# Two expert stages of one kernel: a threshold search shared between VectorE and ScalarE, and the last expert's tail cut into halves

## The reference

```python
T = b * s                                   # 2048 tokens
C = int(T * F_C / E)                        # 256 places for each of 16 experts
scores = softmax(flat_x @ gate_w.T).T       # 16 x 2048
topk_weight, topk_idx = top_k(scores, C)    # the 256 best tokens of each expert
xg = flat_x[topk_idx]
h = gelu(xg @ Wg) * (xg @ Wu)               # 512 inner features
eo = (h @ Wd) * topk_weight
out = zeros.at[topk_idx].add(eo)
shared = (gelu(x @ Sg) * (x @ Su)) @ Sd     # 256 inner features, for all tokens
return out + shared                         # x = x + 0.5 * this
```

## Time and profile before

| | us |
|---|---|
| median of 3 runs | 1262.27 |
| lowest and highest of them | 1257.03, 1264.00 |
| the profiled execution, its own time | 1254.24 |
| its span, first to last instruction | 1252.4 |
| mean granted clock of TensorE, share of full | 0.962 |

### The profile page before, as it was taken

How to read it: one execution, slowest core, us unless ns; L and a number is a source line. 1 busy time by engine, 2 the same in 40 slices (tenths; PEclk the granted TensorE clock), 3 DMA queues, 4 the chain that set the end, 5 groups by cost and what they waited for, 6 DMA issues and landing times. The chain is left out here.

```text
span 1252.4 us, 19707 instructions
## 1 busy us (share of the span) xinstructions
PE 1143.5 (91%) x6507; PEld 567.8 (45%) x6507; DVE 857.6 (68%) x1893; ACT 702.6 (56%) x885; POOL 520.0 (42%) x544
## 2 busy tenths in 40 slices
PE   4799999999999998769997599999999999787998
PEld 1444444444444485358983122222222223446896
DVE  6466566666666555864425999999999995485441
ACT  3677777787787715312215266766777767531221
POOL 0066656656656700337862013223312311135884
PEclk9999999999999998879999599999999999797999
DMA  4001001001001010416754431322222130223765
GB/s 124 1 7 25 18 24 40 18 24 34 24 24 35 19 35 2 171 58 175 188 112 88 88 64 27 73 55 47 57 52 61 42 52 1 84 90 92 196 168 121
DMA packets 54603, 81.90 MB, mean 65 GB/s; under 512 B 18520, under 2 KB 36316, under 8 KB 53404
## 3 DMA queue, kind: packets, MB, share of 16 engines
q1 hardware_dynamic: 42392, 70.83, 21.1%
q0 software_dynamic: 10944, 8.92, 4.8%
q10 hardware_dynamic: 1192, 1.19, 0.3%
HBM read 55.34 MB, written 11.67 MB: 54 GB/s over the span
## 5 line engine op out<-in xcount | busy, mean ns | idle before, releaser
L1777 ACT ACTIVATE at_PR<-psum 128x1024 f32<-128x1024 f32 x256 | 248.0, 1021 | 123.3 <-PE psum L2006 123.0
L1845 DVE TENSOR_REDUCE at_MX<-psum 128x1 f32<-128x512 f32 x468 | 300.9, 685 | 11.0 <-PE psum L1988 6.6
L1714 POOL TENSOR_TENSOR at_PR<-at_PR,at_FAC 128x512 f32<-128x512 f32 x64 | 81.2, 1268 | 293.4 <-ACT at_PR L1777 293.4
L486 ACT ACTIVATE PR<-psum 128x1024 f32<-128x1024 f32 x144 | 141.0, 1026 | 82.1 <-PE psum L770 75.2
L770 PE MATMUL psum<-Q,K 64*128 64x512 f32 (+3 forms) x768 | 143.5, 502 | 1.2 <-ACT PR L486 1.2
L491 ACT ACTIVATE PR<-PR 128x1024 f32<-128x1024 f32 x144 | 144.5, 1062 | 0.0
L782 PE MATMUL psum<-PR,V 128*64 128x512 f32 (+3 forms) x768 | 139.7, 495 | 0.1
L2006 PE MATMUL psum<-at_QS,at_KS 122*128 122x512 bf16 x512 | 136.0, 387 | 2.2 <-DVE at_MX L1841 1.6
L2024 PE MATMUL psum<-at_PR,at_VG 128*32 128x512 f32 x1024 | 137.0, 608 | 0.0
L463 POOL TENSOR_SCALAR_AFFINE_SELECT PR<-PR 128x256 f32<-128x256 f32 (+1 forms) x112 | 58.1, 533 | 167.4 <-ACT PR L491 167.3
L1397 PE MATMUL psum<-moe_XGT,moe_WE 128*128 128x256 f32 x512 | 124.3, 388 | 0.6 <-ACT moe_XGT L1110 0.6
(11 more groups left out here) (238 smaller groups left out, 1629.4 us busy)
## 6 DMA issues: line engine op xcount, KB each, us to landing
moe_WE<-in_c_We SPq DMA_DIRECT2D x32, 768.0 KB
XB<-at_r_dram SPq DMA_DIRECT2D x32, 256.0 KB, 3.8
at_QS<-at_SPL SPq DMA_DIRECT2D x72, 64.0 KB
at_KS<-at_SPL SPq DMA_DIRECT2D x72, 64.0 KB
at_KS<-in_c_krows SPq DMA_DIRECT2D x8, 384.0 KB
moe_rows_dram<-XNS SPq DMA_DIRECT2D x2, 1152.0 KB, 10.4
moe_spare_dram<-moe_zeros SPq DMA_DIRECT2D x2, 1024.0 KB, 13.0
moe_sum_dram<-XB SPq DMA_DIRECT2D x2, 1024.0 KB, 3.8
```

Source lines behind the costliest of these rows:

```text
L486: act.activation(PR[u][:, :, :], S[(b + u) % 2][:, :, :], ACT.Tanh, scale=SCALE0 / CLAMP).then_inc(z.clamped, 1)
L1714: pool.tensor_tensor(pr, pr, FAC[:, 4 * (s // 2):4 * (s // 2) + 4, :], ALU.mult).then_inc(z.factored, 1)
L1777: act.activation(PR[:, gu % PRS, 2 * r:2 * r + 2, :].rearrange("p h n -> p (h n)"), g.psum[:, 2 * r * BANK:(2 * r + 2) * BANK], ACT.Exp).t ...
L1845: dve.tensor_reduce(MX[:, 4 * (2 * pair + c % 2) + I % 4, khalf:khalf + 1], bank(("max", c))[:, :], AX, ALU.max).then_inc(z.reduced, 1)
```

## The change

Five things. (1) ACT counts the third candidate (which is now the middle one in size) as the sum of signs of score minus candidate, over `S3`, a copy of the scores with the lowest bit set; scores are lifted by 2^26, and the candidate carries the sign bit as a negative bias. PE adds ACT's sum with a matrix of halves, after an offset product (`lifted`) in the same PSUM columns, which alternate between two banks. DVE counts two candidates. In step 0 alone DVE has two more passes: it makes `S3`, and counts the scores above zero (a fourth column). (2) Four `shared_in` stand ahead of the turn of the scores; the other twelve stand behind steps 0 to 7 (two behind even steps, one behind odd), `shared_x` and `shared_down` behind steps 8 to 14 and one part behind the search. ACT's Gelu, Copy and halving stand behind its sign of a given step; POOL's pieces may begin three steps earlier. (3) The last down product is made by halves of the inner features and leaves its two halves of rows in two banks, each with its own signal. (4) The mask products take one half of the rows after the other. (5) For quarters 2 and 3 of the tokens DVE and POOL add `LAST` to `g.X` (`merge`), and PE has two L1437 products instead of four.

```diff
+MULTIPLES, SIGN = np.array([1, 3, 2]), np.int64(-2 ** 31)
+LIFT = 26
...
+        def merge(eng, k, done):
+            eng.wait_ge(z.reloaded[k], 16)
+            eng.wait_ge(z.spared[k], 16)
+            eng.tensor_tensor(g.X[:, 4 * k:4 * k + 4, :], g.X[:, 4 * k:4 * k + 4, :], LAST[:, 4 * k:4 * k + 4, :], ALU.add).then_inc(done, 1)
...
             @block.gpsimd
...
-                    pool.wait_ge(z.stepped, o + 5)
+                    pool.wait_ge(z.stepped, o + 2)
...
+                merge(pool, 3, z.merged2)
...
             @block.scalar
...
+                gelu_at, copy_at, half_at = {1: 1, 4: 2, 7: 3}, {0: 0, 3: 1, 5: 2, 8: 3}, {10: 0, 12: 1, 14: 2}
+                shared_gelu(0)
+                act.wait_ge(z.odd, 1)
+                for i in range(SEARCH_STEPS):
+                    act.wait_ge(z.stepped, i + 1)
+                    with nc.allow_low_precision(reason="even integers up to 256"):
+                        act.activation(junk[:, TRIES - 1, :], S3[:, :], ACT.Sign, bias=cand[:, TRIES - 1:TRIES].bitcast(F32),
+                                       accum_out=cnt[:, TRIES - 1:TRIES]).then_inc(z.acted, 1)
+                    if i in gelu_at:
+                        shared_gelu(gelu_at[i])
+                    if i in copy_at:
+                        shared_copy(copy_at[i])
+                    if i in half_at:
+                        shared_half(half_at[i])
+                shared_half(3)
...
             @block.vector
...
-                ch(dve.tensor_copy(S2[:, :], ps[3][:, 0:CW]))
+                ch(dve.tensor_scalar(S2[:, :], ps[3][:, 0:CW], 2.0 ** LIFT, None, ALU.mult))
...
-                    for k in range(TRIES):
+                    for k in range(TRIES - 1):
                         last = dve.tensor_scalar(junk[:, k, :], S2[:, :], cand[:, k:k + 1].bitcast(F32), 0.0, ALU.is_ge,
                                                  ALU.add, accum_out=cnt[:, k:k + 1])
+                        if i == 0 and k == 0:
+                            dve.tensor_scalar(S3[:, :].bitcast(I32), S2[:, :].bitcast(I32), 1, None, ALU.bitwise_or).then_inc(z.odd, 1)
+                    if i == 0:
+                        last = dve.tensor_scalar(junk[:, TRIES, :], S2[:, :], 2.0, 0.0, ALU.is_ge, ALU.add,
+                                                 accum_out=cnt[:, TRIES:TRIES + 1])
...
-                rows_out(E1 - 1)
+                dve.wait_ge(z.scattered[lane(E1 - 1 - DEEP)], landed(E1 - 1 - DEEP))
+                dve.wait_ge(z.wcopied, E1)
+                for k in range(2):
+                    dve.wait_ge(z.down, E1 + k)
+                    dve.tensor_scalar(EO[:, (E1 - 1) % DEEP, k, :], ps[k][:, 0:D], WT[:, (E1 - 1) % DEEP, k:k + 1],
+                                      None, ALU.mult).then_inc(z.scaled, 1)
+                merge(dve, 2, z.merged)
...
             @block.tensor
...
+                for o in range(4):
+                    shared_in(o)
+                pe.wait_ge(z.permuted, 1)
...
+                lifted(0)
                 for i in range(SEARCH_STEPS):
+                    pe.wait_ge(z.acted, i + 1)
+                    pe.matmul(totals(i)[:, TRIES - 1:TRIES], g.half[:, :], cnt[:, TRIES - 1:TRIES], start=False, stop=False,
+                              skip_group_check=True)
                     pe.wait_ge(z.counted, i + 1)
...
-                    pe.matmul(ps[3][:, 256:256 + TRIES], same[:, :], cnt[:, :], start=True, stop=True).then_inc(z.totalled, 1)
+                    pe.matmul(totals(i)[:, 0:TRIES - 1], same[:, :], cnt[:, 0:TRIES - 1], start=False, stop=True,
+                              skip_group_check=True).then_inc(z.totalled, 1)
+                    if i + 1 < SEARCH_STEPS:
+                        lifted(i + 1)
+                    k = (i - 8) // 2
+                    if i < 8:
+                        for o in range(4 + (3 * i + 1) // 2, 4 + (3 * i + 4) // 2):
                             shared_in(o)
+                    elif i % 2 == 0:
...
                         shared_x(k)
                         shared_down(k, 0, 2)
+                    else:
                         shared_down(k, 2, 4)
...
+                shared_down(3, 2, 4)
...
-                down(E1 - 1)
+                pe.wait_ge(z.scaled, 2 * E1 - 2)
+                for h in range(2):
+                    pe.wait_ge(z.hidden, 2 * E1 - 1 + h)
+                    for k in range(2):
+                        last_down(h, k)
                 pe.wait_ge(z.masked, 9)
-                pe.wait_ge(z.scaled, 2 * E1)
-                for t in range(NT):
-                    for k in range(2):
+                for k in range(2):
+                    pe.wait_ge(z.scaled, 2 * E1 - 1 + k)
+                    for t in range(NT):
...
-                for k in range(4):
+                for k in range(2):
                     pe.wait_ge(z.reloaded[k], 16)
                     pe.matmul(ps[4 + k], g.ident[:, :], LAST[:, 4 * k:4 * k + 4, :].rearrange("p t d -> p (t d)"),
                               start=False, stop=False, skip_group_check=True)
                 for k in range(4):
-                    pe.wait_ge(z.spared[k], 16)
+                    if k < 2:
+                        pe.wait_ge(z.spared[k], 16)
+                    else:
+                        pe.wait_ge(z.merged if k == 2 else z.merged2, 1)
```

More of the change, by code:

```diff
@@ L958, in stage_experts @@
     z.masked, z.copied, z.copied2, z.written = (sem(n + "_" + x) for x in "masked copied copied2 written".split())
-    z.resummed, z.table, z.kept = (sem(n + "_" + x) for x in "resummed table kept".split())
+    z.merged, z.merged2 = sem(n + "_merged"), sem(n + "_merged2")
+    z.resummed, z.table, z.kept, z.acted, z.odd = (sem(n + "_" + x) for x in "resummed table kept acted odd".split())
     rows_dram = nc.dram_tensor(f"{n}_rows_dram", [TOK, ROW], F32).ap()
@@ L1008, in stage_experts, with totals @@
         spreads = [ps[f % 2][:, BANK // 2:BANK // 2 + 2 * PART] for f in range(QUARTERS)]
+        def totals(i):
+            return ps[2 + i % 2][:, CW:CW + (TRIES + 1 if i == 0 else TRIES)]
+        def merge(eng, k, done):
+            eng.wait_ge(z.reloaded[k], 16)
+            eng.wait_ge(z.spared[k], 16)
+            eng.tensor_tensor(g.X[:, 4 * k:4 * k + 4, :], g.X[:, 4 * k:4 * k + 4, :], LAST[:, 4 * k:4 * k + 4, :], ALU.add).then_inc(done, 1)
         lists = [ps[f % 2][0:A16 * PART, 0:A16 * PART] for f in range(QUARTERS)]
@@ L1094, in _, with shared_half @@
                     act.activation(SU[:, k % 2, :], g.psum[:, 6 * BANK:8 * BANK], ACT.Copy).then_inc(z.shareducopy, 1)
-                for k in range(4):
+                def shared_half(k):
                     act.wait_ge(z.shareddown, k + 1)
@@ L1136, in _ @@
                 for k in range(TRIES):
-                    last = dve.memset(cand[:, k:k + 1], (k + 1) << (DIGIT * (SEARCH_STEPS - 1)))
+                    value = int(MULTIPLES[k]) << (DIGIT * (SEARCH_STEPS - 1))
+                    last = dve.memset(cand[:, k:k + 1], value if k < TRIES - 1 else value - 2 ** 31)
                 last.then_inc(z.stepped, 1)
@@ L1298, in _ @@
                     mm.then_inc(z.logits, 1)
[L1299 to L1303, removed]
                 def shared_in(o):
@@ L2158, in build @@
         g.same, g.lower = sb("same", [P, P], BF16), sb("lower", [P, P], BF16)
+        g.half, g.offset = sb("half", [P, P], BF16), sb("offset", [P, TRIES + 1], BF16)
         g.units, g.moves = sb("units", [P, SEARCH_STEPS]), sb("moves", [P, SEARCH_STEPS, TRIES], I32)
@@ L2166, in build @@
         g.constants = [(g.gate[:, :], "c_gate"), (g.same[:, :], "c_same"), (g.lower[:, :], "c_lower"),
+                       (g.half[:, :], "c_half"), (g.offset[:, :], "c_shift"),
                        (g.units[:, :], "c_units"), (g.moves[:, :, :], "c_moves"), (g.iota[:, :], "c_iota"),
@@ L2207, in arrays @@
     a["c_units"] = np.tile(unit.astype(np.float32), (P, 1))
-    following = np.append(unit[1:], 0)[:, None] * np.arange(1, TRIES + 1)
-    a["c_moves"] = np.tile((unit[:, None] ^ following).astype(np.int32), (P, 1, 1))
+    following = np.append(unit[1:], 0)[:, None] * MULTIPLES
+    moves = unit[:, None].astype(np.int64) ^ following
+    moves[:, TRIES - 1] ^= SIGN
+    a["c_moves"] = np.tile(moves.astype(np.int32), (P, 1, 1))
+    a["c_half"] = (0.5 * same).astype(HOST_BF16)
+    a["c_shift"] = np.tile(np.array([0, 0, CW, 0]).astype(HOST_BF16), (P, 1))
     a["c_iota"] = np.tile(np.repeat(np.arange(A16), PART).astype(np.float16), (P, 1))
```

41 lines of the change are left out of this document (25 added, 16 removed).

## The result

| | before | after |
|---|---|---|
| median of 20 runs each, side by side, us | 1258.95 | 1262.6 |
| lowest and highest | 1253.51, 1264.16 | 1259.65, 1268.37 |
| the profiled execution, its own time | 1254.24 | 1268.37 |
| its span | 1252.4 | 1266.6 |
| mean granted clock | 0.962 | 0.954 |

The ratio of after to before is 1.0034, with a 95% interval of [1.0022, 1.0046]: 3.7 us slower by the medians, where 4.8 us less was forecast. The profiled execution of after is the longest of its 20. Some 7.7 us of the 14.2 us between the two spans lie in stages whose code is the same (the first expert stage begins at 506.5 instead of 500.0 us); the two expert stages together take 337.6 us instead of 331.1.

What follows compares the result with a forecast made beforehand. The prediction took the search's DVE, PE, DVE chain of waits, 2.215 us a step, to bound each expert stage. 2 x (-4.85 + 1.85) + 1.2 = -4.8 us gave 1257.5 us from 1262.27; range 1250.8 to 1263.5.

Steps and rivals of the forecast that it cites:

- the sentence on POOL: Search: POOL's eight pieces of 1273 ns have steps of 1.8 us and may begin earlier; cost nil.
- (D): Rival: ACT changes tables between Sign and Gelu in the search, +12.3 us, in all 7.5 us slower, 1269.8; chance 0.05.
- The search: Expert stages: one DVE count fewer in 15 steps, -6.00, +0.80 for step 0, +0.35 for PE: -4.85 us a stage.
- pairs: Search steps with two shared_in on PE: 1.87 us against DVE's 1.815; 0.05 a step, seven steps +0.35 us.
- The sign: ACT's count of one candidate in the search: 0.51 us, plus 0.04 semaphore and 0.1 to 0.25 read of the sum.
- the cover: ACT's count ready 0.65 to 0.80 us after the candidates, under DVE's two counts ending at 0.93; cost nil.
- step 0: Start of the search: two DVE passes come back, the fourth count and the making of S3; +0.80 us a stage.
- The late turn: Stage start: four shared_in at the lower clock delay the turn of the scores by 2.05 us; taken as +1.85 a stage.
- My judgment of the early products: Stage start: early work warms the clock, but the cold products themselves are the cost, a price the change doesn't need.
- The end: End of the experts: halves and fewer products gain nil, since PE then waits 3.4 us for the transfer of g.X.
- the merges: End of the experts: additions on POOL and DVE for quarters 2 and 3 fit; cost nil, 0.3 us at most.
- the clock: End of the second stage: clock may fall in PE's wait, slowing the last products; between 0 and +3.4, taken as +1.2 us.

Runs made afterwards that it cites:

- e1: Changed kernel with POOL's eight product pieces beside the search cut from 512 columns to one; 1252.36 us, ratio to the kernel before 0.9967.
- e8: Kernel before with one wait altered, so POOL's pieces start at the end of DVE's three counts instead of with them; 1265.55 us, ratio 1.0081.
- e6: e5 with a search step's two exclusive-ors made one instruction on two alternating rows of candidates; 1254.08 us, ratio to the kernel before 0.9988.
- e7: e6 with the four early shared_in taken apart, one ahead of the scores' turn, the rest spread behind it; 1250.27 us, ratio to before 0.9979.
- e9: e6 with two shared_in ahead of the turn of the scores and two right behind it; 1248.59 us, ratio to the kernel before 0.9936.
- e10: e9 with two products that nobody reads put into PE's wait ahead of the g.X products; 1248.04 us, ratio to the kernel before 0.9940.
- e5: Changed kernel with each POOL piece begun right behind the new candidates, so it lies under DVE's two counts; 1253.80 us, ratio to before 0.9986.
- e4: Kernel before with only the new end of the experts added; 1255.28 us, ratio to the kernel before 0.9995.
- e2: Changed kernel with the search's two exclusive-ors as operations with one tensor and a one-column operand; 1261.55 us, ratio to the kernel before 1.0047.
- e3: Changed kernel's new search with the end of the experts from the kernel before; 1259.33 us, ratio to the kernel before 1.0027.

## Why the prediction was wrong

**The step that failed** is the sentence on POOL: "POOL's eight pieces of 1273 ns have steps of 1.8 us and may begin earlier; nil." I asked whether POOL had time enough, and not what DVE does beside a piece. Before, the wait for the step's signal put each piece under the three counts, which aren't held, and it is just as long as they are (1.27 against 1.30 us). The change shortened that cover to 0.90 us, so a piece that begins with the step now holds `cx`. And it let pieces start earlier: in each stage three of the eight begin when ACT's copy ends, and these met `cand` twice and `cx` once; the piece behind each of them holds another. Half of the question was to be read in the trace of before: the 192 ns of `cx`. What was put at nil costs 6.6 us in the traces of after and e1, and some 8.4 us by the ratios (0.9967 against 1.0034), with the pair at 1.2 GHz in it; e8 shows the hold in the old code by one wait. The forecast's error by the medians, 4.8 + 3.7 = 8.5 us, is not the hold alone: the traces have some 1.2 us more for the turn, 1.6 for that pair and 0.8 for the end. None of my rivals had this mechanism; the slower one (D) was a table load, and the trace has no load beside Sign.

**The rest of the sum stood.** The search of 33.67 - 4.85 = 28.82 us was measured in e1 as 28.80, and steps without a piece take 1.81 us (forecast 1.82), pairs 1.91 (forecast "up to 1.9"; 0.1 a step rather than my 0.05). The sign takes 508 ns (forecast 0.51) and its read of the sum 189 ns (taken as 0.1 to 0.25): the cover held. That the sum comes out to 0.02 us is in part luck: fourteen steps were 0.2 us dearer than forecast, and step 0, with the making of `S3` at 0.29 us instead of 0.40, as much cheaper. With the hold taken away, e1's ratio of 0.9967 stands beside the forecast's 1249.4/1254.24 = 0.9962.

**The late turn was undersized.** Forecast +1.85 us a stage, measured +2.4 and +2.5 in after and e1, +1.4 and +2.5 in e6. The clock rose 4.8 and 5.0 us after PE's first product in after, not 3.4, and the turn stood 5.9 us behind the memset in the second stage, not 5.1. The time of the rise varies: 2.9 us in e6's first stage, 4.9 in its second. And a consequence was not in the sum: in the gap behind the turn the clock fell again in after's second stage, 1.6 us of search for the first pair. In the same gap in e6 it did not fall.

**My judgment of the early products was half right.** They do delay the turn, but e7 shows that taking them away gives the gain back in cold pairs. What pays in the traces is to have the turn in their midst: e9 has the copy 1.2 and 2.2 us earlier than e6 and loses at most 0.6 us of it in a search.

**The end: right but for the merges.** `g.X` lands when POOL's last scatter lets it, and PE waits 3.47 us (forecast 3.4). The last eight records take 1.8 us more than before. By e10 and e5, which have this end at the full clock (4.26 and 4.28 us), some 0.7 of that is the wait for the merges (forecast nil, 0.3 at most) and 1.1 the clock (forecast between 0 and 3.4, taken as 1.2). e4's 0.9995 [0.9974, 1.0017] can't tell +1.2 us from nothing.

**Open.** PE waits 1.88 us between the turn and the first sum of counts. The clock fell right behind that wait in the second stages of after, e2, e3 and e5, and held in their first stages and in both of e1 and e6. What decides it was not tried, nor why it fell later in the searches of e2 and e3.

## What to carry to other kernels

A short instruction on the critical chain of DVE costs what lies beside it on POOL: look up when each POOL instruction starts and ends relative to it, and look at the maximum of its durations, not only at the median. A wait that looks too strict (POOL waiting for `stepped`) can be what keeps two engines apart; loosening it needs the same working as adding work. When work is put in early to bring TensorE's clock up, its place relative to the instruction that others wait for matters: here two products ahead of it and two right behind it did better in the traces than four ahead of it, and better than thinly spread ones.

## What the runs showed of the hardware

- A POOL operation of 128x512 (1.27 us) holds a DVE operation of three integers a partition for up to its whole length, in the form with two tensors (1255 ns) and in the form with one tensor and a one-column operand (1262 ns). Not held were the counts with a sum (472 to 481 ns throughout), the comparison out of PSUM (147 to 163 ns), and an operation of one element a partition (212 to 216 ns).
- ACT's Sign with a sum and a one-column bias takes 508 ns for 128x256, its read of the sum 189 ns (DVE's takes 85), and no table load stood between it, Gelu and Copy in the searches; the two of 1283 ns in the expert stages stand ahead of the first Gelu, as before.
- Two exclusive-ors in one instruction take 222 ns against 161 for one.
- The granted clock rose 2.9 to 6.0 us after PE's first product where four products of 128x512 stood ahead of the turn (after, e1, e2, e3, e5, e6), and 12.7 and 13.1 us after it in e7, where they were spread.
